# A graph network on one core: the five VectorE instructions of a step's block operands, whole or in halves

## The chip, the core and the metric

The kernel runs on one core of one Trainium2 chip. The metric is device time in microseconds for one execution of the whole program; lower is better. Before the change the median of three runs is 948.86 us (948.36 to 949.64).

## The reference, cut to what matters

Four graph layers run one after the other on 3125 nodes with 128 features. The list has 53,125 edges, sorted by destination. Layer 0 computes a message per edge and sums it by destination; layers 1 to 3 sum node rows over the same edges, unweighted in layers 1 and 3 and weighted by `edge_weight` in layer 2.

```python
h = jnp.maximum(_layernorm(x), 0.0)
msg_in = jnp.concatenate([x[src], x[dst], edge_attr], axis=-1)        # layer 0, x here is h
msgs = jnp.maximum(msg_in @ mW1 + mb1, 0.0) @ mW2 + mb2
agg = jax.ops.segment_sum(msgs, dst, num_segments=num_nodes)          # and so on, an MLP and a norm
...
aggr = jax.ops.segment_sum(gathered, edge_dst, num_segments=n)        # layer 1: x @ W1 + b1 + aggr @ W2 + b2
msgs = norm[:, None] * xw[row]                                        # layer 2: norm = dinv[row] * ew * dinv[col]
agg = jax.ops.segment_sum(x[src] * norm[:, None], dst, num_segments=n)  # layer 3, norm from counts alone
```

## The kernel before, in words

The program has three stages. First a set-up loads and normalises the nodes, multiplies them by the message weights (the table `p_rows` in device memory) and sorts out the edges. Then comes **the sweep** over the edges, 104 steps `q` of 512 edges ("quads"). Last comes the dense stage, in which layers 1 to 3 are products of node rows with dense matrices of edge counts and weights, built during the sweep.

A step of the sweep does two jobs.

- **Messages of layer 0.** GpSimd issues four indirect DMAs (`rows_at`, L769), each of which gathers 128 rows of `p_rows` into one of six buffers `G`. It waits only for a buffer to come free. TensorE's `pre(q)` (L1714, L1715) waits for the four gathers, adds the rows up with the destination's part; ScalarE applies a relu (L927); TensorE's `seg(q)` (L1728) sums the messages by destination with a one-hot matrix from VectorE (`onehot`, L1276); VectorE adds the result into `ST` (`add`, L1263).
- **Blocks of the dense matrices.** For step `u = q - 4` of 100, `block_operands(u)` on VectorE makes the operands of eight blocks, in bf16: a mask `mov[:, k, 0]` that compares block columns (L1287), a mask `sta` that compares block rows (L1290), and three products of the first mask with parts of the edge weights (L1294). They lie in one of three sets `k`. TensorE's `blocks(u, 0)` and `blocks(u, 1)` (L1745, L1747) multiply four blocks each; ScalarE reads them (L952, L957) and they are stored. VectorE makes the operands of `u` in its iteration `q = u + 2`, and TensorE uses them in its iteration `q = u + 4`.

From q = 57 on, TensorE, ScalarE and VectorE also do the rest of layer 0 in pieces (`piece_A`, `piece_U`, `piece_V`, L1760 to L1774), one piece in every four steps. The order on each engine is written out by hand; engines meet at semaphores. `s_bop` counts the block operands that are ready and `s_wmm` the halves that TensorE has used. Before the change, `link` puts a wait on VectorE's own semaphore `s_dve` behind the first mask.

A last part, `again`, runs the layers in another way for edge lists that the sweep can't take; it is jumped over for these inputs.

Of the kernel before, what the change touches and what calls it, by code (L numbers as in the profile page):

```python
# [5 lines left out]
def gnn_kernel(nc, x_in, src_in, dst_in, ea_in, ew_in, mW1, mb1, mW2, mb2, uW1, ub1, uW2, ub2,  # L6
# [4 lines left out]
    ALU = mybir.AluOpType  # L11
# [7 lines left out]
    NT = -(-N // 128)  # L19
# [4 lines left out]
    PARTS = 3  # L24
# [7 lines left out]
    PAD_DST = 3135  # L32
# [11 lines left out]
    STEPS = NP // 32  # L44
    CB = 8
    NW = CB // 2
    KCOLS = 4 * NT
# [44 lines left out]
    with ctx:  # L92
# [3 lines left out]
        def sem(name):  # L96
            return ctx.enter_context(nc.semaphore(name))
# [258 lines left out]
        s_R = sem("messages_ready")  # L356
        s_seg = sem("quad_in_psum")
        s_add = sem("quad_added")
        s_bop = sem("block_operands")
        s_cev = sem("counts_read")  # L360
        s_wmm = sem("weights_in_psum")
# [156 lines left out]
        def _(sp):  # L518
# [165 lines left out]
            with sp.Else():  # L684
                sp.dma_start(x[:, 0:NT - 1, :], x_in[0:128 * (NT - 1), :].rearrange("(t p) d -> p t d", p=128))\
                    .then_inc(s_xc[0], 16)
                sp.wait_ge(z_set, 1)
                sp.dma_start(x[0:NR, NT - 1, :], x_in[128 * (NT - 1):N, :]).then_inc(s_xc[0], 16)
                for i in range(2):
                    sp.dma_start(z_wc[:, i, :], mW1[2 * D + i:2 * D + i + 1, :].to_broadcast([128, D])).then_inc(z_ld, 16)  # L690
                sp.dma_start(z_mb, mb1.rearrange("(a d) -> a d", a=1).to_broadcast([128, D])).then_inc(z_ld, 16)
                whole_c = E // 128
                for c0 in range(0, whole_c, 64):
                    c1 = min(c0 + 64, whole_c)
                    for to, of in ((z_dsti, dst_in), (z_w, ew_in)):
                        sp.dma_start(to[:, c0:c1], of[128 * c0:128 * c1].rearrange("(c p) -> p c", p=128),
                                     allow_slow_non_contiguous=True)\
                            .then_inc(z_ld, 16)
                    sp.dma_start(z_ea[:, c0:c1, :], ea_in[128 * c0:128 * c1, :].rearrange("(c p) i -> p c i", p=128))\
# [12 lines left out]
                sp.dma_start(deg_tab[0:1, 0:NP], ST[0:1, :]).then_inc(s_dst4, 16)  # L712
                sp.dma_start(deg_tab[1:2, 0:NP], ST[1:2, :]).then_inc(s_dst4, 16)
                sp.dma_start(deg_tab[2:3, 0:NP], invb[0:1, :]).then_inc(s_dst4, 16)
                sp.dma_start(deg_tab[3:4, 0:NP], aggT[0:1, :]).then_inc(s_dst4, 16)
                sp.wait_ge(s_dst4, 128)
                load_degrees(sp, 1)
                for s, tile, ready in ((2, h, s_rows[2]), (3, h, s_rows[3]), (4, g3, s_rows[4])):
                    sp.wait_ge(ready, seen(s, 1, NC - 1))
                    sp.dma_start(row_tabs[s].rearrange("(t p) d -> p t d", p=128), tile[:, :, :])\  # L720
                        .then_inc(z_kst, 16)
                store_out(1)
# [3 lines left out]
        def _(pool):  # L726
# [64 lines left out]
                    .then_inc(s_lo, 1)  # L791

            pool.wait_ge(s_oh, NQ)
            pool.wait_ge(s_bop, STEPS)
            widen_group(1, 0)
            pool.wait_ge(s_pre, NQ)
            widen_group(1, 1)
# [48 lines left out]
        def _(act):  # L846
# [270 lines left out]
            with act.Else():  # L1117
                act.wait_ge(s_out, 16 * NC)
                pipeline((0, root(0, 1)), (1, rows(0, 1, h, ACT.Relu, x)), (2, read_T0(1)), (3, store_P_again))
                for j in range(NC):  # L1120
                    act.wait_ge(mm["Q"], j + 1)
                    if j >= 2:
                        act.wait_ge(z_qst, 16 * j)
                    act.activation(z_st[:, j % 2, 0:width(j)], bank(6 + j % 2, width(j)), ACT.Copy).then_inc(ev["Q"], 1)

                def again_sums(s):
                    for j in range(NC):
                        act.wait_ge(z_mm, (s + 1) * NCH + 1)
                        act.activation(part_of(ST, j), bank(j, width(j)), ACT.Copy).then_inc(z_acc, 1)

                again_sums(0)
                again_sums(1)
                layer0()
                again_sums(2)
                pipeline((0, root(3, 1)), (1, rows(3, 1, h, ACT.Relu, x)))
                again_sums(3)
                pipeline((0, root(4, 1)), (1, scaled_rows(1)))
                for j in range(NC):
                    late_part(1, j)
                again_sums(4)  # L1140

        @block.vector
        def _(dve):
            links = [0]

            def link(ins):
                links[0] += 1
                ins.then_inc(s_dve, 1)
                dve.wait_ge(s_dve, links[0])
# [126 lines left out]
                    last = dve.tensor_scalar(oh[:, q % OS, c, :], iota[:, :], dstT[:, q, c:c + 1], None, ALU.is_equal)  # L1276
                last.then_inc(s_oh, 1)

            def blocks_of(a, u, n):
                return a[:, CB * u:CB * u + CB].rearrange("p (i a t) -> p i a t", a=1, t=2)\  # L1280
                    .to_broadcast([128, NW, n, 2])

            def block_operands(u):
                if u >= SETS:
                    dve.wait_ge(s_wmm, 2 * (u - SETS + 1))
                k = u % SETS
                link(dve.tensor_tensor(mov[:, k, 0, :, :, :],  # L1287
                                       iota_k[:, :, :].rearrange("p (a c) t -> p a c t", a=1)
                                       .to_broadcast([128, NW, KCOLS, 2]), blocks_of(Kt, u, KCOLS), ALU.is_equal))
                dve.tensor_tensor(sta[:, k, :, :, :],  # L1290
                                  iota_l[:, :, :].rearrange("p (a c) t -> p a c t", a=1)
                                  .to_broadcast([128, NW, 128, 2]), blocks_of(LOt, u, 128), ALU.is_equal)
                for a in range(PARTS):
                    last = dve.tensor_tensor(mov[:, k, 1 + a, :, :, :], mov[:, k, 0, :, :, :],  # L1294
                                             blocks_of(Wp[:, a, :], u, KCOLS), ALU.mult)
                last.then_inc(s_bop, 1)

            def unpack():
                dve.wait_ge(s_win, 16 * GROUPS)
# [285 lines left out]
                dve.sem_inc(z_set, 1)  # L1585
            with dve.Else():
                dve.wait_ge(s_out, 16 * NC)
                dve.memset(x[:, NT - 1, :], 0.0).then_inc(z_set, 1)
                dve.memset(z_dsti[:, NCH - 1:NCH], PAD_DST).then_inc(z_set, 1)
                dve.memset(z_w[:, NCH - 1:NCH], 0.0).then_inc(z_set, 1)  # L1590
                dve.memset(z_ea[:, NCH - 1:NCH, :], 0.0).then_inc(z_set, 1)
                dve.wait_ge(s_xc[0], 48)
                pipeline((0, variance(0, 1, x)), (1, norm(0, 1)))
                dve.wait_ge(z_ld, 16 * NLOADS)
                dve.wait_ge(z_set, 5)
                link(dve.tensor_copy(z_dstf, z_dsti))
                link(dve.memset(z_R, 0.0))
                link(dve.memset(z_R[:, 0:1], 1.0))
# [48 lines left out]
        def _(pe):  # L1647
# [82 lines left out]
                last.then_inc(s_seg, 1)  # L1730

            def blocks(u, hh):
                if hh == 0:
                    pe.wait_ge(s_bop, u + 1)
                    if u == 0:
                        pe.wait_ge(s_kev, 3)
                        pe.wait_ge(s_flag, 1)
                if u >= 1:
                    pe.wait_ge(s_cev, 2 * u + hh - 1)
                    pe.wait_ge(s_wev, 2 * u + hh - 1)  # L1740
                k = u % SETS
                for b in range(NW):
                    i, t = (NW * hh + b) // 2, b % 2
                    lo, to = sta[:, k, i, :, t], block_out(hh)[:, b, 0:2 * KCOLS]
                    pe.matmul(to.rearrange("p (a c) -> p a c", a=2), lo, mov[:, k, 0:2, i, :, t], start=True, stop=False)  # L1745
                    for a in range(1, PARTS):
                        weighed = pe.matmul(to[:, KCOLS:2 * KCOLS], lo, mov[:, k, 1 + a, i, :, t],  # L1747
                                            start=False, stop=a == PARTS - 1)
                weighed.then_inc(s_wmm, 1)
# [272 lines left out]
```

## Time and profile before

| | |
|---|---|
| median of 3 runs | 948.86 us (948.36 to 949.64) |
| span of the profiled execution | 946.8 us |
| outside the span, against the median | 2.1 us |
| sweep: first gather to last `seg` | about 41 to 624 us |
| TensorE, share of the span | 90% |
| VectorE | 67% |
| ScalarE | 54% |
| GpSimd | 55% |

Of the profiled execution only the span is known; its own time outside the profile is taken as that of the three runs. A view of groups gives, for each line of the kernel, the busy time, the mean duration of one instruction, and the idle time before it with what ended that idle time. The chain of waits is followed back from the end of the program, so it says what set the time at each moment. On VectorE consecutive instructions overlap by some 0.08 us in the records, so what one costs the engine is the distance between two starts, which is less than its duration.

### The profile page before, as it was taken

The page shows a single profiled execution, that of the slowest core. Times are in us where ns is not written, and L with a number is a line of the kernel's source. Part 1 is how long each engine was busy: PE and PEld are TensorE (multiplying, and loading weights), DVE is VectorE, ACT ScalarE, POOL GpSimd, SP SyncE. Part 2 cuts the span into 40 slices and gives each one's busy share as a digit, 9 for nine tenths or more (in the row PEclk, how much of TensorE's full clock was granted, in tenths as well). Part 3 has the DMA queues.
Part 4 walks back from the last instruction along what each step waited for, and adds up shares of the span by engine and source line. Part 5 has one row for each costly group of instructions (what it writes and reads, how often), then busy time and mean ns, then how long its engine had stood idle before and what let it go on. Part 6 is the DMA issues. An engine that isn't in the chain of part 4 may idle for free.

```text
span 946.8 us, 19062 instructions
## 1 busy us (share of the span) xinstructions
PE 851.2 (90%) x6997; PEld 788.9 (83%) x6997; DVE 636.1 (67%) x1758; ACT 510.7 (54%) x1013; POOL 520.9 (55%) x496
## 2 busy tenths in 40 slices
PE   3257889889898978999989999999999999999997
PEld 2257879879898978989989999987889888888886
DVE  6528979887786877779897989968743311115664
ACT  2224757556575656768777788853353011114873
POOL 5477777777777777777777777745110000023110
PEclk9667999999898989999999999999999999999999
DMA  8752556556565666556565556656247778784500
GB/s 206 199 109 71 159 160 209 165 159 214 174 200 158 173 142 192 165 165 204 168 184 156 176 159 196 176 172 195 70 157 274 295 297 299 297 287 139 165 23 27
DMA packets 109503, 168.91 MB, mean 178 GB/s; under 512 B 14723, under 2 KB 69545, under 8 KB 109406
## 3 DMA queue, kind: packets, MB, share of 16 engines
q1 hardware_dynamic: 92062, 137.01, 44.8%
q0 software_dynamic: 13648, 28.21, 11.5%
q10 hardware_dynamic: 3696, 2.42, 0.9%
q8 instruction: 59, 0.97, 0.4%
q14 instruction: 38, 0.31, 0.1%
HBM read 109.15 MB, written 58.44 MB: 177 GB/s over the span
## 4 chain that ended last, share of the span: by engine, by line
PE 43%; POOL 38%; issue 13%; DMA 4%; ACT 1%; SPq 1%; DVE 1%; ACTq 0%; POOLq 0%; DVEq 0%
POOL room L769 36%; PE ps L1889 14%; PE ps L1874 14%; PE ps L1714 2%; DMA room<-p_rows,idx 2%; PE ps L1715 2%; PE ps L1728 2%; PE ps L1858 2%; PE ps L1745 2%; PE ps L1747 2%; PE ps L1650 1%; DMA w_m<-in_L_gnn_mW 1%; POOL pair L769 1%; DMA p_rows<-g 1%; ACTq L905 0%
## 5 line engine op out<-in xcount | busy, mean ns | idle before, releaser
L769 POOL DMA_INDIRECT room<-p_rows,idx x416 | 438.0, 1053 | 137.5 <-issue 125.0
L1714 PE MATMUL ps<-room,ident 128*128 128x128 f32 x832 | 178.8, 299 | 59.7 <-DMA room<-p_rows,idx 58.9
L1714 PEld LDWEIGHTS ps<-room,ident 128*128 128x128 f32 x832 | 135.5, 205 | 63.5 <-DMA room<-p_rows,idx 45.6
L1715 PE MATMUL ps<-room 128*128 128x128 f32 x832 | 170.6, 289 | 0.0
L1745 PE MATMUL ps<-room 128*128 128x200 bf16 x800 | 161.3, 253 | 0.0
L1747 PE MATMUL ps<-room 128*128 128x100 bf16 x1600 | 160.6, 208 | 0.0
L1294 DVE TENSOR_TENSOR room<-room,Wp 128x800 bf16<-128x800 bf16 x300 | 155.4, 571 | 0.0
L1747 PEld LDWEIGHTS ps<-room 128*128 128x128 bf16 x1600 | 147.9, 98 | 3.9
L1889 PE MATMUL ps<-room,h 128*128 128x256 f32 (+1 forms) x650 | 136.2, 371 | 0.0
L1715 PEld LDWEIGHTS ps<-room 128*128 128x128 f32 x832 | 136.0, 205 | 0.0
L927 ACT ACTIVATE g<-ps 128x512 f32<-128x512 f32 x104 | 62.2, 598 | 136.8 <-PE ps L1715 136.7
L1889 PEld LDWEIGHTS ps<-room,h 128*128 128x128 f32 x650 | 119.2, 190 | 15.2
L952 ACT ACTIVATE room<-ps 128x400 uint8<-128x400 f32 x200 | 100.1, 501 | 34.6 <-PE ps L1747 31.9
L1728 PE MATMUL ps<-g 128*128 128x128 f32 x832 | 117.6, 285 | 0.0
L1874 PE MATMUL ps<-wide_room,parts 128*128 128x512 f32 (+1 forms) x520 | 114.7, 375 | 0.0
L1874 PEld LDWEIGHTS ps<-wide_room,parts 128*128 128x128 f32 x520 | 91.1, 188 | 18.1 <-POOL wide_room L474 0.9
L1728 PEld LDWEIGHTS ps<-g 128*128 128x128 f32 x832 | 102.4, 194 | 0.0
L957 ACT ACTIVATE room<-ps 128x400 f32<-128x400 f32 x200 | 100.6, 503 | 0.0
L1263 DVE TENSOR_TENSOR ST<-ST,ps 128x128 f32<-128x128 f32 x104 | 29.1, 279 | 104.8 <-PE ps L1701 70.7
L1276 DVE TENSOR_SCALAR g<-iota,dstT 128x128 f32<-128x128 f32 x416 | 92.2, 299 | 0.0
L870 ACT ACTIVATE sd<-mv,eps 128x2 f32<-128x2 f32 (+3 forms) x45 | 13.5, 301 | 140.2 <-DVE mv L1164 140.2
L933 ACT ACTIVATE room<-room,npio 125x512 bf16<-125x512 bf16 x104 | 75.7, 728 | 17.3 <-DMA room<-dst_row 17.3
(195 smaller groups left out, 1132.1 us busy)
## 6 DMA issues: line engine op xcount, KB each, us to landing
weight_blocks<-room SPq DMA_DIRECT2D x50, 800.0 KB, 4.6
room<-weight_blocks SPq DMA_DIRECT2D x12, 3200.0 KB
room<-dst_row SPq DMA_DIRECT2D x52, 256.0 KB
room<-count_blocks SPq DMA_DIRECT2D x8, 1600.0 KB
count_blocks<-room SPq DMA_DIRECT2D x50, 200.0 KB
room<-p_rows,idx POOLq DMA_INDIRECT x416
first_c<-count_blocks SPq DMA_DIRECT2D x4, 1600.0 KB, 10.0
edge_windows<-room SPq DMA_DIRECT2D x1, 3072.0 KB
```

The costliest lines, as they stand in the source:

```text
L769: return pool.indirect_dma_start(to, None, table, bass.IndirectOffsetOnAxis(ap=at, axis=0))
L952: act.activation(cnt_out[:, u % OUTS, :, at16].rearrange("p h (b w) -> p b h w", w=4), of, ACT.Copy)\
L957: act.activation(w_out[:, u % OUTS, :, at16].rearrange("p h (b w) -> p b h w", w=4), of, ACT.Copy)\
L1276: last = dve.tensor_scalar(oh[:, q % OS, c, :], iota[:, :], dstT[:, q, c:c + 1], None, ALU.is_equal)
L1294: last = dve.tensor_tensor(mov[:, k, 1 + a, :, :, :], mov[:, k, 0, :, :, :], blocks_of(Wp[:, a, :], u, KCOLS), ALU.mult)
L1714: pe.matmul(to, ident[:, :], G[:, n % GS, c, :], start=True, stop=False)
L1715: last = pe.matmul(to, sT[:, n % TS, 128 * c:128 * c + 128], Qr[:, n % QS, :], start=False, stop=True)
L1728: last = pe.matmul(bank(2 + n % 2, 128), R[:, n % RS, c, :], oh[:, n % OS, c, :], start=c == 0, stop=c == 3)
L1745: pe.matmul(to.rearrange("p (a c) -> p a c", a=2), lo, mov[:, k, 0:2, i, :, t], start=True, stop=False)
L1747: weighed = pe.matmul(to[:, KCOLS:2 * KCOLS], lo, mov[:, k, 1 + a, i, :, t], start=False, stop=a == PARTS - 1)
L1874: last = pe.matmul(to, Hr[:, t, a, :], at[:, k, 0:n], start=a == 0 and t == 0, stop=a == 1 and t == NT - 1)
L1889: last = pe.matmul(bank(dense_bank(j))[:, 256 * half:256 * half + 32 * c], h[:, t, :], ring_w[(2 * j + half) % 3][:, 0:c, t, :], start=t = ...
```

## The change

Each of the five instructions becomes two, over four blocks each. Their order is: first mask for half 0, for half 1; second mask for half 0, for half 1; three products of half 0; three products of half 1. Both first masks count up a new semaphore, and the products of a half wait for the mask of their half; the wait between the first and the second mask is gone. `s_bop` is counted up twice in a step, and each of TensorE's `blocks(u, hh)` waits for its own half. The semaphores of the part that is jumped over are renumbered, without effect here.

```diff
+        s_mask = sem("block_masks")
...
-            pool.wait_ge(s_bop, STEPS)
+            pool.wait_ge(s_bop, 2 * STEPS)
...
-                k = u % SETS
-                link(dve.tensor_tensor(mov[:, k, 0, :, :, :],
-                                       iota_k[:, :, :].rearrange("p (a c) t -> p a c t", a=1)
-                                       .to_broadcast([128, NW, KCOLS, 2]), blocks_of(Kt, u, KCOLS), ALU.is_equal))
-                dve.tensor_tensor(sta[:, k, :, :, :],
...
-                for a in range(PARTS):
-                    last = dve.tensor_tensor(mov[:, k, 1 + a, :, :, :], mov[:, k, 0, :, :, :],
-                                             blocks_of(Wp[:, a, :], u, KCOLS), ALU.mult)
-                last.then_inc(s_bop, 1)
+                k, h2 = u % SETS, NW // 2
+                halves = [slice(h2 * half, h2 * half + h2) for half in range(2)]
...
+                for at in halves:
+                    dve.tensor_tensor(mov[:, k, 0, at, :, :],
...
+                        .then_inc(s_mask, 1)
+                for at in halves:
+                    dve.tensor_tensor(sta[:, k, at, :, :],
...
+                for half, at in enumerate(halves):
+                    dve.wait_ge(s_mask, 2 * u + half + 1)
+                    for a in range(PARTS):
+                        last = dve.tensor_tensor(mov[:, k, 1 + a, at, :, :], mov[:, k, 0, at, :, :],
+                                                 blocks_half(Wp[:, a, :], KCOLS, at), ALU.mult)
+                    last.then_inc(s_bop, 1)
...
             def blocks(u, hh):
+                pe.wait_ge(s_bop, 2 * u + hh + 1)
                 if hh == 0:
-                    pe.wait_ge(s_bop, u + 1)
```

On VectorE, one step in the middle of the sweep is this before the change (`room` is the memory that holds `mov` and `sta`; `quad_added`, `q_window_in_psum`, `messages_in_psum` and `quad_in_psum` are semaphores of the message job, `weights_in_psum` is `s_wmm`, `dve_chain` is `s_dve`):

```order
L1263 TENSOR_TENSOR ST<-ST,ps 128x128 [waits quad_added,q_window_in_psum]
L1270 COPY room<-ps 125x128 [waits messages_in_psum,q_window_in_psum]
L1276 TENSOR_SCALAR g<-iota,dstT 128x128 [waits quad_in_psum]
L1276 TENSOR_SCALAR g<-iota,dstT 128x128 x3
L1287 TENSOR_TENSOR room<-iota_k,Kt 128x800 [waits weights_in_psum]
L1290 TENSOR_TENSOR room<-iota_l,LOt 128x1024 [waits dve_chain]
L1294 TENSOR_TENSOR room<-room,Wp 128x800 x3
```

The same step of VectorE after the change, where lines have moved by 2 to 9:

```order
L1265 TENSOR_TENSOR ST<-ST,ps 128x128 [waits quad_added,q_window_in_psum]
L1272 COPY room<-ps 125x128 [waits messages_in_psum,q_window_in_psum]
L1278 TENSOR_SCALAR g<-iota,dstT 128x128 [waits quad_in_psum]
L1278 TENSOR_SCALAR g<-iota,dstT 128x128 x3
L1292 TENSOR_TENSOR room<-iota_k,Kt 128x400 [waits weights_in_psum]
L1292 TENSOR_TENSOR room<-iota_k,Kt 128x400
L1297 TENSOR_TENSOR room<-iota_l,LOt 128x512 x2
L1303 TENSOR_TENSOR room<-room,Wp 128x400 [waits block_masks]
L1303 TENSOR_TENSOR room<-room,Wp 128x400 x2
L1303 TENSOR_TENSOR room<-room,Wp 128x400 [waits block_masks]
L1303 TENSOR_TENSOR room<-room,Wp 128x400 x2
```

Five instructions with one wait on the engine itself have become ten with two such waits, at a later place; nothing else of the step has moved.

On TensorE, this is `seg` with what follows it and the start of the second half, before the change:

```order
L1728 MATMUL ps<-g 128x128 [waits quad_added,q_window_ready,onehot_ready,messages_ready]
L1728 MATMUL ps<-g 128x128 x3
L1701 MATMUL ps<-w_m,hT 128x128
L1745 MATMUL ps<-room 128x200 [waits weights_read,counts_read]
L1747 MATMUL ps<-room 128x100 x2
```

And after it:

```order
L1737 MATMUL ps<-g 128x128 [waits quad_added,q_window_ready,onehot_ready,messages_ready]
L1737 MATMUL ps<-g 128x128 x3
L1710 MATMUL ps<-w_m,hT 128x128
L1754 MATMUL ps<-room 128x200 [waits weights_read,counts_read,block_operands]
L1756 MATMUL ps<-room 128x100 x2
```

The order is the same; the first product of the second half has a third semaphore to wait for.

## Rows read from the trace of the kernel before

**Rows 1.** Page, parts 1 and 4: busy time of engines, the chain that ended last.

```profile
PE 851.2 (90%) x6997; PEld 788.9 (83%) x6997; DVE 636.1 (67%) x1758; ACT 510.7 (54%) x1013; POOL 520.9 (55%) x496
...
PE 43%; POOL 38%; issue 13%; DMA 4%; ACT 1%; SPq 1%; DVE 1%; ACTq 0%; POOLq 0%; DVEq 0%
```

**Rows 2.** Chain of waits around the end of the sweep: start us, us, what.

```profile
489.22 0.30 issue
489.53 7.50 DMA room<-p_rows,idx
...
506.82 0.96 PE ps L1728 x8
...
527.66 0.96 PE ps L1728 x8
...
613.12 4.20 DMA room<-p_rows,idx
617.37 0.49 PE ps L1714 x2
```

**Rows 3.** Who waited for whom: engine, line, releaser, us in total, times, longest.

```profile
POOL room L769 <- issue: 125.0, 410, 0.3
...
PE ps L1714 <- DMA room<-p_rows,idx: 58.9, 19, 16.4
...
POOL room L769 <- PE ps L1715: 1.5, 5, 0.3
```

**Rows 4.** GpSimd's groups, stretch 70 to 366, then 366 to 614.1.

```profile
L769 POOL DMA_INDIRECT room<-p_rows,idx x216 | 231.1, 1070 | 65.8 <-issue 64.3 <-PE ps L1715 1.5
```

```profile
L769 POOL DMA_INDIRECT room<-p_rows,idx x185 | 192.2, 1039 | 56.4 <-issue 56.4
```

**Rows 5.** Line L769: duration ns, min, median and max.

```profile
L769 POOL DMA_INDIRECT room<-p_rows,idx x416: 941/947/3783, 40.8 to 613.1; - x139
```

**Rows 6.** VectorE in order of time: start us, us, instruction.

```profile
222.49 0.69 DVE L1290 TENSOR_TENSOR room<-iota_l,LOt 128x1024 bf16<-128x1024 bf16 x1
223.10 1.54 DVE L1294 TENSOR_TENSOR room<-room,Wp 128x800 bf16<-128x800 bf16 x3
...
225.59 0.86 DVE L1276 TENSOR_SCALAR g<-iota,dstT 128x128 f32<-128x128 f32 x4
226.37 0.57 DVE L1287 TENSOR_TENSOR room<-iota_k,Kt 128x800 bf16<-128x800 bf16 x1
226.97 0.69 DVE L1290 TENSOR_TENSOR room<-iota_l,LOt 128x1024 bf16<-128x1024 bf16 x1
227.58 1.54 DVE L1294 TENSOR_TENSOR room<-room,Wp 128x800 bf16<-128x800 bf16 x3
```

**Rows 7.** GpSimd in the same stretch.

```profile
222.90 1.11 POOL L769 DMA_INDIRECT room<-p_rows,idx  x1 [0.31 <-issue]
224.31 1.15 POOL L769 DMA_INDIRECT room<-p_rows,idx  x1 [0.30 <-issue]
225.76 0.95 POOL L769 DMA_INDIRECT room<-p_rows,idx  x1 [0.30 <-issue]
227.01 1.47 POOL L769 DMA_INDIRECT room<-p_rows,idx  x1 [0.30 <-issue]
```

**Rows 8.** Chain of waits, three long gathers of GpSimd.

```profile
237.07 1.82 POOL room L769
...
313.37 3.78 POOL room L769
...
334.58 3.66 POOL room L769
```

**Rows 9.** TensorE in order of time, two steps in a row.

```profile
296.36 1.12 PE L1728 MATMUL ps<-g 128*128 128x128 f32 x8
300.84 1.12 PE L1728 MATMUL ps<-g 128*128 128x128 f32 x8
```

**Rows 10.** Engines' busy time in 500 to 600: PE, PEld, DVE, ACT, POOL, clock, DMA.

```profile
500.00:600.00 100.00, 100.00 (x1036) 95.32 (x1036) 87.08 (x279) 80.37 (x178) 77.30 (x75) 1.00 0.57 172
```

**Rows 11.** VectorE's waits in 500 to 600.

```profile
DVE ST L1263 <- PE ps L1767: 8.9, 5, 5.6
DVE ST L1263 <- PE ps L1761: 4.5, 5, 0.9
```

More of the change, by code:

```diff
@@ L686, in _ @@
                     .then_inc(s_xc[0], 16)
-                sp.wait_ge(z_set, 1)
+                sp.wait_ge(s_pad, 11)
                 sp.dma_start(x[0:NR, NT - 1, :], x_in[128 * (NT - 1):N, :]).then_inc(s_xc[0], 16)
@@ L1131, in _ @@
                 again_sums(0)
+                act.wait_ge(s_dst4, 128)
                 again_sums(1)
@@ L1277, in onehot @@
                 last.then_inc(s_oh, 1)
-            def blocks_of(a, u, n):
-                return a[:, CB * u:CB * u + CB].rearrange("p (i a t) -> p i a t", a=1, t=2)\
-                    .to_broadcast([128, NW, n, 2])
             def block_operands(u):
@@ L1285, in block_operands, with blocks_half @@
                     dve.wait_ge(s_wmm, 2 * (u - SETS + 1))
-                k = u % SETS
-                link(dve.tensor_tensor(mov[:, k, 0, :, :, :],
-                                       iota_k[:, :, :].rearrange("p (a c) t -> p a c t", a=1)
-                                       .to_broadcast([128, NW, KCOLS, 2]), blocks_of(Kt, u, KCOLS), ALU.is_equal))
-                dve.tensor_tensor(sta[:, k, :, :, :],
-                                  iota_l[:, :, :].rearrange("p (a c) t -> p a c t", a=1)
-                                  .to_broadcast([128, NW, 128, 2]), blocks_of(LOt, u, 128), ALU.is_equal)
-                for a in range(PARTS):
-                    last = dve.tensor_tensor(mov[:, k, 1 + a, :, :, :], mov[:, k, 0, :, :, :],
-                                             blocks_of(Wp[:, a, :], u, KCOLS), ALU.mult)
-                last.then_inc(s_bop, 1)
+                k, h2 = u % SETS, NW // 2
+                halves = [slice(h2 * half, h2 * half + h2) for half in range(2)]
+                def blocks_half(a, n, at):
+                    return a[:, CB * u + 2 * at.start:CB * u + 2 * at.stop].rearrange("p (i a t) -> p i a t", a=1, t=2)\
+                        .to_broadcast([128, h2, n, 2])
+                for at in halves:
+                    dve.tensor_tensor(mov[:, k, 0, at, :, :],
+                                      iota_k[:, :, :].rearrange("p (a c) t -> p a c t", a=1)
+                                      .to_broadcast([128, h2, KCOLS, 2]), blocks_half(Kt, KCOLS, at), ALU.is_equal)\
+                        .then_inc(s_mask, 1)
+                for at in halves:
+                    dve.tensor_tensor(sta[:, k, at, :, :],
+                                      iota_l[:, :, :].rearrange("p (a c) t -> p a c t", a=1)
+                                      .to_broadcast([128, h2, 128, 2]), blocks_half(LOt, 128, at), ALU.is_equal)
+                for half, at in enumerate(halves):
[4 more added lines that the diff above has]
+                    last.then_inc(s_bop, 1)
             def unpack():
@@ L1587, in _ @@
                 dve.wait_ge(s_out, 16 * NC)
[L1588 to L1591, printed above, removed]
+                dve.memset(x[:, NT - 1, :], 0.0).then_inc(s_pad, 1)
+                dve.memset(z_dsti[:, NCH - 1:NCH], PAD_DST).then_inc(s_pad, 1)
+                dve.memset(z_w[:, NCH - 1:NCH], 0.0).then_inc(s_pad, 1)
+                dve.memset(z_ea[:, NCH - 1:NCH, :], 0.0).then_inc(s_pad, 1)
                 dve.wait_ge(s_xc[0], 48)
@@ L1594, in _ @@
                 dve.wait_ge(z_ld, 16 * NLOADS)
-                dve.wait_ge(z_set, 5)
+                dve.wait_ge(z_set, 1)
                 link(dve.tensor_copy(z_dstf, z_dsti))
```

## The prediction

> **What bounds the kernel now.** I began with the page. TensorE is busy for 90% of the span and VectorE for 67%, yet the chain that ended last gives TensorE only 43% of the span, and GpSimd's work 38% with 13% of "issue" beside it [rows 1]. So in about half of the span the time is set by GpSimd, which does little else there than issue the gathers. The waits say the same from the other side: TensorE stood 58.9 us for gathered rows to land, GpSimd stood 1.5 us in all for a free buffer, and 125.0 us of its idle time is a fixed 0.30 us between two gathers [rows 3]. GpSimd therefore runs through the sweep at its own pace. No wait of TensorE for a VectorE product of the blocks is among the costly ones; the operands are made in iteration u + 2 and used in u + 4.
>
> The chain around the sweep's end has three pieces [rows 2]: GpSimd up to a gather issued at 489.53 that took 7.50 us, then TensorE from step to step, and at the end again the last gather, issued at 613.12, which took 4.20 us and for which TensorE's last `pre` waited until 617.37. TensorE's own pace is 4.48 us a step before q = 57 (300.84 - 296.36) [rows 9] and (527.66 - 506.82) / 4 = 5.21 us with the pieces of layer 0 [rows 2]. GpSimd's pace is (231.1 + 65.8) / 54 = 5.50 us a step in 70 to 366, and (192.2 + 56.4) / 46.25 = 5.38 in 366 to 614 [rows 4]. The slower of the two is GpSimd in both parts: by 1.0 us a step in the first, but by only 0.16 in the second, that is 7.6 us over 46 steps.
>
> **What GpSimd waits for.** A gather takes 0.947 us in the median, but 1.070 and 1.039 in the mean [rows 4, 5]: 26.5 us (231.1 - 216 x 0.947) and 17.0 us (192.2 - 185 x 0.947) beyond the median. Beside VectorE's times [rows 6, 7] a pattern shows. The gather of 222.90 begins while L1290 (to 223.18) runs, and ends at 224.01, 0.83 behind it. That of 224.31 begins within the last L1294 (to 224.64) and ends 0.82 behind it. That of 227.01 meets L1290 (to 227.66) and ends 0.82 behind it, though the next VectorE instruction began at 227.58. That of 225.76, among the short L1276, took 0.95. So a gather that starts within such a VectorE instruction stands until this one instruction ends, then needs 0.82 us; it is let through between two in a row. It waits if the instruction has more than 0.947 - 0.82 = 0.13 us left.
>
> The Trainium skill, SBUF — State Buffer, "Who interferes with whom", says that a VectorE instruction with two SBUF inputs blocks a GpSimd instruction that reads SBUF, for the whole instruction; the trace agrees in these rows, where both inputs are in SBUF.
>
> **The change, part by part.**
>
> *GpSimd.* An instruction of duration d has a window of d - 0.13 in which a gather's start is held, on average by half of it, so the wait goes with the square of the window. Before: four of 0.44 (0.57 - 0.13) and one of 0.56 (0.69 - 0.13): (4 x 0.19 + 0.31) / 2 = 0.54. Half the size: 224 columns are 0.12 to 0.13 us (0.69 - 0.57), so 400 fewer take 0.22 off and 512 fewer 0.29: 0.35 and 0.40 long, windows 0.22 and 0.27. After: (8 x 0.048 + 2 x 0.073) / 2 = 0.27. The waits on these instructions halve.
> How large are they? From 43.5 us I take what longer instructions cause: the two gathers of 3.78 and 3.66 (5.5 us), and those like the 1.82 one, of which there are four as `block_degrees` runs four times (3.5 us) [rows 8]. That leaves 17.5 in the first part and 17.0 in the second. The four L1276 (0.28 each, windows of 0.15) have 0.05 against 0.54, some 10%. So 15.7 and 15.3 us hang on the five, and halving saves 7.8 and 7.6, together **15.4 us of GpSimd's time**.
>
> *VectorE.* From the starts in [rows 6]: L1290 costs 0.61 us (226.97 to 227.58), the first mask 0.60 with its wait (226.37 to 226.97), and three L1294 in 1.54 - 0.57 are 0.485 apart. Extrapolated from 800 and 1024 columns the fixed cost of one is 0.485 - 800 x 0.125 / 224 = 0.04 us. It can't be under nothing, and the nearest short row is L1276: (0.86 - 0.28) / 3 = 0.19 for 128 columns of fp32 all told, the upper bound. I take 0.04 to 0.07. Five more instructions are 0.2 to 0.35 us a step; the dropped wait gives 0.11 back (0.60 - 0.485). Net +0.1 to +0.24 us. Its cover is VectorE's idle time. In 500 to 600 it is 87% busy [rows 10] and waits 13.4 us, of which one wait of 5.6 belongs to the late gather; the other 7.8 us over the 18 steps are 0.43 a step [rows 11]. So 0.2 is left, and cost nothing. In the first part the pace leaves TensorE 1.0 us a step, and VectorE, which follows it, has that on top.
> The Trainium skill, Perfetto Trace Analysis, "Optimizing Scalar/DVE Operations", speaks against the change: some 60 ns of overhead for each VectorE instruction, so rather grouped. By its figure, an estimate, VectorE's step would grow by 5 x 0.06 - 0.11 = 0.19 us, within my range and under the idle time.
>
> *TensorE.* One more semaphore on 100 products that already wait for two. The halves come earlier, but TensorE wasn't waiting. I take 0; bounds 0 and 0.05 us a step.
>
> *The sum.* First part: TensorE is far from its limit, so all 7.8 us arrive. Second part: GpSimd would come to 5.38 - 7.6 / 46 = 5.21, level with TensorE. At best it gives 7.6. But when both have one pace, a gather that lands late is not made up for: that of 489.53 was 3.3 us later than the last one (7.50 against 4.20), which before was hidden by the 0.16 us a step. At worst it gives 7.6 - 3.3 = 4.3. So 12.1 to 15.4, I take 13.4. Against the profiled span that is 946.8 to 933.4; with the 2.1 us between span and median, 948.9 to **935.5 us**. The dense stage, some 320 us behind the sweep, is not touched.
>
> **The rivals.**
>
> *No change in GpSimd's waits (about 949).* The wait could go with the time for which VectorE holds what both want, not with one instruction: then two halves hold it as long as the whole. For it: I have it from a few coincidences. Against it: at 227.01 GpSimd got in between two instructions with no gap between them. VectorE's extra 0.1 to 0.24 us stays hidden, so 948 to 951.
> The Trainium skill, SBUF — State Buffer, in the same section, infers that descriptor generation needs only the write side, so that `tensor_tensor` would not stall it; by that the split would give nothing, and the rows on 1.11 and 1.47 us speak against it.
>
> *The gain ends up in TensorE (about 943).* If further late gathers or a lower granted clock take the second part's gain and some of the first's, 4 to 7 us remain: 942 to 945. For it: TensorE is 100% busy in 500 to 600 [rows 10]. Against it: in the first part it has 1 us a step to spare.
>
> *VectorE becomes the bound (slower, about 965).* The mechanism is a fixed cost per instruction near the upper bound, 0.19. The step grows by 5 x 0.19 - 0.11 = 0.84, over the 0.43 of idle time: 0.41 x 46 = 19 us over TensorE's 46 x 5.21 = 240, so 259 against 46 x 5.38 = 248, 11 slower. Halves would then last 0.5, GpSimd's windows 0.37 eight times and 0.43 twice, 0.73 against 0.54, and the first part would lose 15.7 x 0.35 = 5.5: some 16 us in all. It decides from (0.43 + 0.11) / 5 = 0.11 us an instruction on. Against it: two sizes of the same instruction give 0.04.
>
> **How the numbers follow.** 0.2% of 949, 1.9 us, is about what a measurement can tell from no change. The forecast (929 to 942) has 0.71. The gain that ends in TensorE has 0.08, no change in the waits 0.12, VectorE as the bound 0.09. Faster: 0.71 + 0.08 = 0.79; same 0.12; slower 0.09. The range begins at 929, since 15.4 us are all that halving can give and some clock and landing times may improve with it, and goes up to 948, which leaves out the slower case, most of "no change" and a little below 929, in all some 0.2.
>
> **What would show it.** The mean of L769 falls from 1053 ns in the page's groups to about 1015, its median stays at 947, no gather among block operands is above 1.25, and GpSimd's last gather is issued near 598 instead of 613. The ten VectorE instructions are 0.35 and 0.40 us long and start 0.26 to 0.28 and 0.32 to 0.34 apart; VectorE still waits for TensorE in 500 to 600, and TensorE never for the block operands. I'd be wrong if L769 keeps its mean, if VectorE's waits are gone, or if the gathers speed up and TensorE's steps grow.

## The result: 1098 us, 16% slower

The changed kernel takes 1098.16 us in the median of 4 runs (1092.3 to 1105.73), against 949.25 for the kernel before in the same comparison. The ratio is 1.156, 95% interval 1.150 to 1.161. I had forecast 935.5 and gave "slower" 0.09. The times below leave out three slow runs: one of `mask_halves` (2180.56 us), one of the kernel before (2989.71 us) and one of `whole_pause_after_copy` (1040.98 us; the ratio of 1.085 in the table counts it, and the medians without it give 1.078).

From the page of the changed kernel: the span, part 1 and a row of part 5, beside [rows 1] (a line may have moved: L769 is L770 now, L1714 is L1723):

```profile
span 1102.1 us, 19562 instructions
...
PE 898.8 (82%) x6997; PEld 828.8 (75%) x6997; DVE 662.5 (60%) x2258; ACT 512.9 (47%) x1013; POOL 671.3 (61%) x496
...
L770 POOL DMA_INDIRECT room<-p_rows,idx x416 | 589.0, 1416 | 137.9 <-issue 124.4
```

The 416 gathers have 589.0 us of GpSimd's time, 1416 ns each. Before, their mean was 1070 ns in the first and 1039 in the second part [rows 4], in all 438.0 us. That is 151.0 us more, of the 155.3 by which the span grew, and the last gather is issued at 764.97 instead of 613.12 [rows 2], 151.9 us later:

```profile
764.97 3.52 DMA room<-p_rows,idx
768.54 0.49 PE ps L1723 x2
```

The fixed "issue" time between the gathers is as it was [rows 3]. Who waited for whom, and the single gathers (min, median, max in ns):

```profile
PE ps L1723 <- DMA room<-p_rows,idx: 165.4, 54, 17.2
...
L770 POOL DMA_INDIRECT room<-p_rows,idx x416: 940/947/3792, 41.6 to 765.0; - x139
```

TensorE waits 165.4 us for gathered rows, where it waited 58.9 [rows 3], and none of its waits is put down to the block operands. The median gather is 0.947 us as before [rows 5]. So most gathers are as fast as ever and some are very slow.

TensorE's clock fell too. In the sweep, before and after (engines as in [rows 10], the clock behind the five busy times):

```profile
70.00:614.00 544.00, 497.95 (x5104) 482.49 (x5105) 451.43 (x1283) 372.30 (x776) 422.14 (x400) 0.96 0.58 171
```

```profile
70.00:766.00 696.00, 545.56 (x5117) 522.76 (x5117) 478.64 (x1785) 375.35 (x778) 574.02 (x401) 0.89 0.44 134
```

The mean granted clock is 0.89 instead of 0.96, and TensorE's matmuls take 47.6 us more. It is busy for 78% of the stretch instead of 92%, standing still for gathered rows in between, so this slower clock did not set the pace.

GpSimd (first) and VectorE in order of time, beside [rows 6, 7]:

```profile
303.28 0.94 POOL L770 DMA_INDIRECT room<-p_rows,idx  x1 [0.30 <-issue]
304.53 3.30 POOL L770 DMA_INDIRECT room<-p_rows,idx  x1 [0.30 <-issue]
308.14 0.94 POOL L770 DMA_INDIRECT room<-p_rows,idx  x1 [0.30 <-issue]
```

```profile
303.20 1.07 DVE L1278 TENSOR_SCALAR g<-iota,dstT 128x128 f32<-128x128 f32 x4
304.05 0.63 DVE L1292 TENSOR_TENSOR room<-iota_k,Kt 128x400 bf16<-128x400 bf16 x2
304.60 0.75 DVE L1297 TENSOR_TENSOR room<-iota_l,LOt 128x512 bf16<-128x512 bf16 x2
305.27 1.74 DVE L1303 TENSOR_TENSOR room<-room,Wp 128x400 bf16<-128x400 bf16 x6
```

The gather of 304.53 begins within the second half of the first mask. It ends at 307.83. The row of ten block instructions ends at 305.27 + 1.74 = 307.01, and 307.83 is 0.82 behind that. The 0.82 is the time that I had read from [rows 6, 7], but what it counts from is now the end of all ten instructions and not of the one that was met.

### The profile page after: what moved, and what is told of

The parts are those of the page before. It is cut to its first block and busy times, and to the rows that moved or that the text cites. A ratio compares the mean times of both kernels' runs of the same rounds, so it can differ in the third digit from the quotient of the medians.

```text
span 1102.1 us, 19562 instructions
## 1 busy us (share of the span) xinstructions
PE 898.8 (82%) x6997; PEld 828.8 (75%) x6997; DVE 662.5 (60%) x2258; ACT 512.9 (47%) x1013; POOL 671.3 (61%) x496
## 5 line engine op out<-in xcount | busy, mean ns | idle before, releaser
L770 POOL DMA_INDIRECT room<-p_rows,idx x416 | 589.0, 1416 | 137.9 <-issue 124.4
L1723 PE MATMUL ps<-room,ident 128*128 128x128 f32 x832 | 196.2, 323 | 166.1 <-DMA room<-p_rows,idx 165.4
L1723 PEld LDWEIGHTS ps<-room,ident 128*128 128x128 f32 x832 | 149.5, 225 | 175.5 <-DMA room<-p_rows,idx 156.6
L1724 PE MATMUL ps<-room 128*128 128x128 f32 x832 | 186.7, 312 | 0.0
L1303 DVE TENSOR_TENSOR room<-room,Wp 128x400 bf16<-128x400 bf16 x600 | 175.1, 363 | 0.0
L1265 DVE TENSOR_TENSOR ST<-ST,ps 128x128 f32<-128x128 f32 x104 | 29.6, 284 | 236.1 <-PE ps L1710 157.5
L1754 PE MATMUL ps<-room 128*128 128x200 bf16 x800 | 169.4, 262 | 0.0
L1756 PE MATMUL ps<-room 128*128 128x100 bf16 x1600 | 168.6, 213 | 0.0
L1756 PEld LDWEIGHTS ps<-room 128*128 128x128 bf16 x1600 | 153.9, 101 | 6.0
L1724 PEld LDWEIGHTS ps<-room 128*128 128x128 f32 x832 | 151.5, 227 | 0.0
L791 POOL TENSOR_TENSOR parts<-g,parts 128x512 fp32r<-128x512 f32 x5 | 6.4, 1272 | 130.4 <-ACT parts L1051 130.4
L1754 PEld LDWEIGHTS ps<-room 128*128 128x128 bf16 x800 | 81.7, 102 | 3.9 <-issue 3.6
```

The costliest lines, as they stand in the source:

```text
L770: return pool.indirect_dma_start(to, None, table, bass.IndirectOffsetOnAxis(ap=at, axis=0))
L1303: last = dve.tensor_tensor(mov[:, k, 1 + a, at, :, :], mov[:, k, 0, at, :, :], blocks_half(Wp[:, a, :], KCOLS, at), ALU.mult)
L1723: pe.matmul(to, ident[:, :], G[:, n % GS, c, :], start=True, stop=False)
L1724: last = pe.matmul(to, sT[:, n % TS, 128 * c:128 * c + 128], Qr[:, n % QS, :], start=False, stop=True)
```

## The experiments

The ratios below are to the kernel before on the same chip, with 95% intervals. "Waits" is 416 x (mean - 0.944 us), from the row of L769 or L770 of each profile; 0.944 us is the median gather in `halves_two_pauses`, where few are held.

| kernel | ratio | mean gather, ns | waits, us |
|---|---|---|---|
| before | 1 | 1053 | 45 |
| changed | 1.156 (1.150 to 1.161) | 1416 | 196 |
| halves_one_wait | 1.146 (1.139 to 1.152) | 1374 | 179 |
| whole_no_gap | 1.120 (1.114 to 1.125) | 1338 | 164 |
| mask_halves | 1.129 (1.119 to 1.139) | 1359 | 173 |
| product_halves | 1.002 (1.000 to 1.005) | 1056 | 47 |
| group_gaps | 0.996 (0.993 to 0.998) | 1010 | 27 |
| whole_pause_and_wait | 1.001 (0.999 to 1.003) | 1050 | 44 |
| whole_pause_before | 1.018 (1.013 to 1.022) | 1086 | 59 |
| halves_one_pause | 1.009 (1.006 to 1.013) | 1073 | 54 |
| mask2_first | 1.049 (1.044 to 1.054) | 1158 | 89 |
| whole_pause_after_copy | 1.085 (1.079 to 1.091) | 1227 | 118 |
| product_quarters | 1.041 (1.033 to 1.049) | 1154 | 87 |
| halves_two_pauses | **0.977 (0.975 to 0.980)** | 996 | 22 |

The time goes with the waits of the gathers. Each kernel's time differs from that of the kernel before by what its waits differ, within 6 us, `product_quarters` (39 and 42 us) and `whole_pause_before` (16 and 14) included. The exception is `group_gaps`: its waits are 18 us shorter, its time only 6; its VectorE is 97% busy in 500 to 600, against 87% before.

### Is it the size, or the row?

In the diffs `mask1(at)`, `mask2(at)` and `product(a, at)` are the instructions of L1287, L1290 and L1294 over the pairs of blocks `at`; the diffs are to the body of `block_operands` in the kernel before, or in the changed kernel where this is said. Each kernel computes the whole reference.

A "pause" is a wait of VectorE for a result of its own that isn't there yet, so that it stands still for a moment (0.03 us between the masks in [rows 6]). The first kernel leaves every instruction whole and only drops the pause:

```diff
-                link(mask1(whole))
+                mask1(whole).then_inc(s_mask, 2)
                 mask2(whole)
+                dve.wait_ge(s_mask, 2 * u + 2)
                 for a in range(PARTS):
                     last = product(a, whole)
```

> Whole instructions as before, but without the wait between the first and the second mask; the products wait for the mask instead, as in the changed kernel. Theory LINE-UP (a gather that meets a row of VectorE instructions with no pause between them stands until the row ends, once enough of them follow): the row is now five long, a gather caught in the first mask stands up to 2.7 us, the mean gather goes from 1.05 to 1.2 us or more and the time to 990 us or more. Theory SIZE (what keeps a gather out is that the instructions are short; between instructions of 0.56 us or more it gets in): gather mean 1.05 us, longest wait by the block instructions under 0.6 us, time 945 to 951 us.

It took 1068 us. A gather of it and the instructions of VectorE around:

```profile
148.49 3.39 POOL L770 DMA_INDIRECT room<-p_rows,idx  x1 [0.30 <-issue]
```

```profile
148.44 0.57 DVE L1288 TENSOR_TENSOR room<-iota_k,Kt 128x800 bf16<-128x800 bf16 x1
148.92 0.68 DVE L1294 TENSOR_TENSOR room<-iota_l,LOt 128x1024 bf16<-128x1024 bf16 x1
149.53 1.54 DVE L1299 TENSOR_TENSOR room<-room,Wp 128x800 bf16<-128x800 bf16 x3
```

The gather met the whole first mask at 148.49 and ended at 151.88, which is 0.81 behind the end of the last product (151.07). SIZE falls: at 0.57 and 0.68 us the same happens. 116 of the 149 us come without a single halved instruction.

The second and third halve one kind only. `product_halves` keeps the pause behind the first mask; `mask_halves` has none.

```diff
                 mask1(whole).then_inc(s_mask, 2)
                 dve.wait_ge(s_mask, 2 * u + 2)
                 mask2(whole)
-                for a in range(PARTS):
-                    last = product(a, whole)
+                for at in halves:
+                    for a in range(PARTS):
+                        last = product(a, at)
```

> Masks whole with the pause behind the first, as before; only the three products are halved, six in a row behind the second mask. LINE-UP: seven in a row without a pause, so gathers caught in the second mask or the first products stand up to 2.3 us; mean 1.25 us or more, time over 1000 us. SIZE: a gather caught in the second mask gets in behind it, one caught in a product stands to the end of the six, up to 1.7 us; mean near 1.2 us, time 980 to 1020 us. If neither (no gather waits over 0.6 us), the halved masks are what matters.

953 us, the mean gather 1056 ns. Seven instructions in a row follow the pause, and every gather got in behind the one that it met. So both theories were wrong here: how many instructions follow does not decide.

```diff
-                link(mask1(whole))
-                mask2(whole)
+                for at in halves:
+                    mask1(at).then_inc(s_mask, 1)
+                for at in halves:
+                    mask2(at)
+                dve.wait_ge(s_mask, 2 * u + 2)
```

> Both masks halved (four instructions of 0.36 to 0.42 us, no pause), products whole behind them. LINE-UP: seven in a row, as bad as the product halves or worse, over 1000 us. SIZE: a gather caught in a half mask stands to the end of the four, about 1.2 us, and gets in between whole products; mean near 1.1 us, time 955 to 980 us.

1076 us. Its time agrees with LINE-UP, but after `product_halves` that theory could not stand. What the three slow kernels (changed, `whole_no_gap`, `mask_halves`) have in common, and `product_halves` has not, is the lost pause.

`group_gaps` is the changed kernel with a pause behind each group:

```diff
                 for at in halves:
                     mask1(at).then_inc(s_mask, 1)
+                dve.wait_ge(s_mask, 2 * u + 2)
                 mask2(halves[0])
-                mask2(halves[1])
+                link(mask2(halves[1]))
                 for half, at in enumerate(halves):
-                    dve.wait_ge(s_mask, 2 * u + half + 1)
...
                     last.then_inc(s_bop, 1)
+                    dve.wait_ge(s_bop, 2 * u + half + 1)
```

> All ten halves as in the changed kernel, with VectorE waiting for its own last result behind every group (2 first masks, 2 second masks, 3 products, 3 products). LINE-UP with a row of at most three: gathers get in at every boundary, mean 1.0 us, time 935 to 950 us. SIZE: gathers stand to the end of their group, at most 1.0 us; mean 1.06 to 1.1 us, time 945 to 970 us. Either way far below the 1098 us of the changed kernel; if it stays above 1050, the pauses do not matter and both theories fall.

946 us, a little under the kernel before. Four pauses turn 1.156 into 0.996, all ten halves being kept. The waits ahead of the products are gone here too; the next kernel and `halves_one_pause`, which keeps them, show that they are not what counts.

### Where must the pause be, and does a wait in the row matter?

The changed kernel also has a wait that is met in advance, ahead of the products. `whole_pause_and_wait` keeps the pause and adds such a wait:

```diff
-                link(mask1(whole))
-                mask2(whole)
-                for a in range(PARTS):
-                    last = product(a, whole)
+                mask1(whole).then_inc(s_mask, 1)
+                dve.wait_ge(s_mask, 2 * u + 1)
+                mask2(whole).then_inc(s_mask, 1)
+                product(0, whole)
+                dve.wait_ge(s_mask, 2 * u + 2)
+                product(1, whole)
+                last = product(2, whole)
```

> Whole instructions with the pause behind the first mask, as before the change; new is a wait of the second product for the second mask, that is for the instruction but one ahead of it, as the changed kernel's products wait for their mask. Theory PAUSE (gathers get in between VectorE instructions only in a row that VectorE began after standing still; a row that runs on from the one-hots without a pause shuts them out): the gathers are as before, mean 1.05 us, longest by the block instructions under 0.6 us, time 945 to 953 us. Theory MET WAIT (a wait in the row for an earlier instruction of the same row shuts out the gathers that came before it): those caught in the second mask stand to the end of the row, 2 us, mean 1.2 us or more, time over 1000 us.

`whole_pause_before` is `whole_no_gap` with a pause ahead of the first mask:

```diff
+                dve.wait_ge(s_oh, min(u + 4, NQ))
                 mask1(whole).then_inc(s_mask, 2)
                 mask2(whole)
```

> Whole instructions, no pause behind the first mask and the met wait ahead of the products, as in the run that took 1068 us; new is a pause ahead of the first mask, where VectorE waits for its own last one-hot. PAUSE: the row begins after standing still, so gathers get in at every boundary, mean 1.05 us, 945 to 955 us. MET WAIT: nothing is mended, 1040 us or more.

951 and 967 us. The met wait does nothing. The pause works from ahead of the masks too, though this kernel came out above the 945 to 955 expected: only one gather at a block instruction was kept beyond the one that it met, yet the mean is 1086 ns. The gathers that met a product and got in behind it stood 25.6 us in all, against 14.2 before. Why they stood longer is only argued: a gather that is let in behind one instruction begins the next at a fixed distance, and here falls in with a worse phase.

`halves_one_pause` is the changed kernel with one pause put back, between the two first half masks:

```diff
+                mask1(halves[0]).then_inc(s_mask, 1)
+                dve.wait_ge(s_mask, 2 * u + 1)
+                mask1(halves[1]).then_inc(s_mask, 1)
```

> The changed kernel with one thing put back: VectorE waits for the first half mask before the second. All else is as in the changed kernel. PAUSE: a gather caught by any half gets in behind it; mean 0.99 to 1.04 us, longest by the block instructions under 0.5 us, time 935 to 950 us. MET WAIT: gathers caught in the first four instructions are still shut out, over 1040 us.

959 us, so one pause in a step takes 139 of the 149 us away. It missed its range of 935 to 950 by 9.

`mask2_first` is `whole_no_gap` with the masks in the other order, so that the wait of the products is a pause:

```diff
-                mask1(whole).then_inc(s_mask, 2)
                 mask2(whole)
+                mask1(whole).then_inc(s_mask, 2)
                 dve.wait_ge(s_mask, 2 * u + 2)
```

> Whole instructions in the order second mask, first mask, pause (the products wait for the instruction right ahead), products. PAUSE: a gather caught in the first of the row stands to the end of the second, at most 1.1 us; from the pause on it gets in everywhere; mean 1.06 to 1.12 us, time 948 to 975 us. MET WAIT: the wait is one that is not met in advance, as before the change, so about the same prediction, not higher than 975 us. If it comes out over 1020 us both fall: the order or the instruction ahead of the one-hots matters.

994 us, above its range. Of the 44 us by which the waits are longer than before, some 25 are of 31 gathers that met the second mask ahead and stood to the pause behind the first. Another 17 are of gathers that met a product and got in behind it: they stood 31.3 us in all, against 14.2 before.

### Counting in the row

For each gather that met a block instruction with more than 0.13 us left, I looked up in the starts and durations of the trace how many VectorE instructions had run since VectorE last stood still, and whether the gather ended 0.82 us behind the one that it met ("in") or later ("out"). Gathers that were not held at all, the last block instruction of a step and any instruction right ahead of a pause are left out: behind these nothing holds a gather for long, or in and out can't be told apart. So are positions beyond the eleventh.

```
kernel                   position since VectorE stood still: in/out
before                   1: 26/0   3: 22/0
product_halves           1: 64/0   3: 22/0   4: 8/0    6: 68/0
whole_pause_and_wait     1: 28/0   3: 16/0
whole_pause_before       1: 33/0   2: 31/0   3: 7/0    4: 35/1   5: 1/0    10: 1/0
halves_one_pause         1: 12/0   2: 12/0   3: 19/0   4: 43/0   7: 17/6   8: 3/16
group_gaps               1: 39/0   2: 26/0   7: 0/11
mask2_first              2: 9/0    7: 5/7    8: 2/8    9: 2/2    10: 0/14
changed                  3: 1/0    5: 1/1    7: 2/9    8: 0/10   9: 4/21   10: 0/7   11: 0/3
whole_no_gap             2: 1/0    3: 5/0    4: 0/1    7: 4/7    8: 7/14   9: 7/10   10: 4/6   11: 2/0
mask_halves              3: 1/0    4: 1/0    5: 0/1    6: 1/0    7: 13/3   8: 0/5    9: 0/30   10: 0/9   11: 17/4
```

Up to the sixth nearly all got in, from the seventh on most did not; but the 13 of 16 at the seventh in `mask_halves` did. The sixth rests almost wholly on `product_halves`, where only one block instruction is left behind it. In the changed kernel the row begins with `add` (L1265), the copy and four one-hots, so that the first half mask is already the seventh.

The pause also helps at once. Of the 46 gathers of the kernel before that met L1290, the instruction right behind the pause, the 16 that began within 0.041 us of its start were not held at all, and the mask lasted 0.73 to 0.77 us instead of 0.69; those from 0.046 us on with more than 0.13 us of it left were held to its end:

```profile
231.45 0.76 DVE L1290 TENSOR_TENSOR room<-iota_l,LOt 128x1024 bf16<-128x1024 bf16 x1
```

```profile
231.49 0.95 POOL L769 DMA_INDIRECT room<-p_rows,idx  x1 [0.31 <-issue]
```

Three kernels test what the count suggests. The first is `halves_one_pause` with a second pause:

```diff
                     last.then_inc(s_bop, 1)
+                    if half == 0:
+                        dve.wait_ge(s_bop, 2 * u + 1)
```

> The changed kernel with two pauses of VectorE: behind the first half mask and behind the first half's products, so that no row of VectorE instructions without a pause has more than seven, and of its block instructions only the one that a pause follows stands seventh. Theory COUNT (a gather gets in behind the instruction it met if that is among the first six since VectorE last stood still; from the seventh on it mostly stands to the row's end): with one pause, gathers that met the eighth and ninth instruction still stood to the end; here none does, no gather stands over 0.5 us at the block instructions, mean 0.99 to 1.03 us, time 938 to 950 us. Rival (one pause behind the masks is enough and the 959 us with one pause come from VectorE's added time): a second pause costs VectorE 0.1 us more, 958 to 965 us.

931 us: the fastest of all, 2.3% under the kernel before. No gather stood over 0.5 us at a block instruction, as expected; the range of 938 to 950 us was missed by 7, to the good.

`product_quarters` is `product_halves` with four slices in place of two:

```diff
-                for at in halves:
+                for i in range(NW):
                     for a in range(PARTS):
-                        last = product(a, at)
+                        last = product(a, slice(i, i + 1))
```

> Masks whole with the pause behind the first, as before; the three products in quarters, so twelve short ones follow the second mask, thirteen in a row without a pause and without any wait in the row. COUNT (position in the row alone decides): gathers that met one of the first five or six get in behind it, those that met the seventh to tenth stand up to 1.2 us, to the row's end. Rival (a wait inside the row is needed to shut them out; in all rows that did so there was one): every gather gets in behind the instruction that it met, none over 0.6 us at the block instructions. The time says little here, since VectorE has some 0.6 us more a step: 950 to 990 us.

990 us. For the products COUNT holds, and the rival falls. The twelve products begin at 160.90, 0.17 apart; the gather of 162.10 met the seventh of them, the eighth since the pause, and stood until 163.06, the end of the twelve, plus 0.81:

```profile
162.10 1.77 POOL L770 DMA_INDIRECT room<-p_rows,idx  x1 [0.30 <-issue]
```

```profile
160.29 0.69 DVE L1294 TENSOR_TENSOR room<-iota_l,LOt 128x1024 bf16<-128x1024 bf16 x1
160.90 2.16 DVE L1299 TENSOR_TENSOR room<-room,Wp 128x200 bf16<-128x200 bf16 x12
162.98 0.28 DVE L1265 TENSOR_TENSOR ST<-ST,ps 128x128 f32<-128x128 f32 x1
```

VectorE did not stand still behind the twelve: `add` began at 162.98, before the last product had ended. So what ends such a wait is the end of the block instructions, and not a standstill.

All 28 gathers that met the seventh product stood 0.8 us or more, while the 72 that met the third or fourth product (the fourth and fifth since the pause) stood 0.05 at most.

`whole_pause_after_copy` is `whole_no_gap` with a pause in `onehot`:

```diff
             def onehot(q):
+                if q:
+                    dve.wait_ge(s_Qr, min(q + 3, NQ))
                 for c in range(4):
```

> Whole instructions with no pause behind the first mask (that took 1068 us); new is a pause ahead of the four one-hots, well away from the masks. COUNT: the first mask is now the fifth since VectorE stood still and the second the sixth, so gathers that met these get in behind them, where before they stood up to 2.5 us; mean 1.05 to 1.15 us, time 950 to 985 us. Rival (a pause helps only where it is next to the masks): 1040 us or more, waits of 2.5 us remain.

1026 us. Better than without the pause (1068), but far above the 950 to 985 expected. Gathers that met the first mask, the fifth since the pause, got in 24 times and stayed out 10; those at the second mask, the sixth, 1 and 15. So the number is not the whole rule, and a limit of six is not one either. In the kernels without a pause behind the first mask, gathers that met one of the last two or three of the row also got in again: all that met the second product did, 25 at position 8 in `whole_pause_after_copy` and 4 at position 10 in `whole_no_gap`, and in the changed kernel the 4 at position 9 met the ninth half. The count does not explain that, nor that in `product_quarters`, at the products with two or one behind them, 71 of 72 gathers did not. How VectorE and GpSimd pass on what both want is open. What is shown is that taking the standstill away shuts gathers out for whole rows and putting it back lets most of them in. For how many instructions it helps is known only roughly.

### TensorE's part

In the changed kernel:

```diff
-                pe.wait_ge(s_bop, 2 * u + hh + 1)
                 if hh == 0:
+                    pe.wait_ge(s_bop, 2 * u + 2)
```

> The changed kernel, but TensorE waits once a step for both halves. Theory COUNT puts the whole loss on VectorE's instructions and GpSimd's gathers: 1085 to 1110 us as the changed kernel. Rival (TensorE's wait for the second half costs time): clearly below 1085 us.

1091 us in 2 runs, within the 1085 to 1110 expected. The ratio is 1.146 (1.139 to 1.152), and its interval overlaps that of the changed kernel (1.150 to 1.161). Its gathers wait 179 us instead of 196, which is more than the 8 us between the medians. TensorE's second wait is not the cause of the loss; that it costs up to some 1% isn't excluded.

### The version that beats both

`halves_two_pauses` is the changed kernel and two lines that let VectorE wait for itself. Its page, its waits and its busy time in 500 to 600, beside [rows 10]:

```profile
span 929.6 us, 19662 instructions
...
L770 POOL DMA_INDIRECT room<-p_rows,idx x416 | 414.5, 996 | 138.0 <-issue 123.4
```

```profile
PE ps L1736 <- DMA room<-p_rows,idx: 29.3, 14, 4.9
...
PE ps L1767 <- DVE room L1299: 1.5, 1, 1.5
```

```profile
500.00:600.00 100.00, 100.00 (x1046) 96.02 (x1045) 97.65 (x385) 80.66 (x180) 69.24 (x73) 1.00 0.59 178
```

```profile
L770 POOL DMA_INDIRECT room<-p_rows,idx x416: 940/944/4072, 41.4 to 590.2; - x139
```

The gathers have 23.5 us less than before (438.0 - 414.5) and the last is issued at 590.2 instead of 613.1. TensorE waits half as long for them. VectorE is 98% busy in 500 to 600, so nothing is left there for more instructions. The median fell by 21.4 us (952.09 to 930.68).

## Why the prediction was wrong

- **The bound** was right. GpSimd's gathers set the sweep's pace; they account for 151 of the 155 us, and for the gain of `halves_two_pauses` too (23.5 us less in the gathers, 21.4 in the time).
- **The step that failed** is in "What GpSimd waits for": "a gather that starts within such a VectorE instruction stands until this one instruction ends ... it is let through between two in a row". The rows showed it for instructions that stand first to fourth behind a pause [rows 6, 7]; I took it for a rule on any two instructions. Even there it had an exception, the 16 gathers that came right behind the pause. The runs showed instead that it holds for a few instructions after VectorE has stood still, and that later ones mostly keep the gather out to the end of the block instructions. So the term of 15.4 us saved was 151 us lost.
- **The dropped wait** stood in the sum as a saving, "the dropped wait gives 0.11 back". The 0.11 is right (first mask to next instruction 0.60 before, 0.484 in `whole_no_gap`); what it had done for GpSimd was worth some 116 us.
- **Halving the waits.** What the waits cost before was right: by the starts and durations of the trace, gathers that met one of the five instructions stood 31.1 us in all, and the sum has 15.7 + 15.3. What shorter instructions save was too low once the pauses are there: in `halves_two_pauses` 7.6 us of the 31.1 are left, so 23.5 are saved and not 15.4. That this kernel takes 931 us, near my 935.5 for the changed one, is partly luck: it is another kernel, with two pauses that the sum did not have.
- **VectorE's cost.** Starts are 0.276 and 0.334 apart and the halves last 0.36 and 0.42 us; I had 0.26 to 0.28, 0.32 to 0.34, and 0.35 and 0.40. From 0.276 at 400 columns and 0.484 at 800 the fixed cost of one is 2 x 0.276 - 0.484 = 0.07 us, the upper end of my 0.04 to 0.07. It did not become the bound.
- **TensorE's cost** of nothing for the third semaphore was right within some 1%.
- **The rivals.** None named this. "No change in GpSimd's waits" had the thought that what VectorE holds may be more than one instruction, but let it stay at the old sum. The slower rival had the wrong mechanism and a size of 16 us.
- **The page's rule.** In [rows 7] each gather that was held waited for one instruction; later in a row it was for up to ten, 2.8 us. The Trainium skill, SBUF — State Buffer, "Who interferes with whom", lets the loser wait for "the whole instruction". The runs here disagree for gathers that come late in a row. The same section's inference that `tensor_tensor` would not stall descriptor generation does not hold for these gathers: at the five `tensor_tensor` they stood 31.1 us in all before the change, and single ones up to 2.8 us after it.

## What to carry to other kernels

When an engine gets what it shares with another only between the other's instructions, look at what stands between these before you remove it: a wait that costs 0.1 us may be the gap through which the other engine lives. Before splitting an instruction, count how many run in a row without a standstill, and put a pause back after some five. Its place has to be tried: ahead of the one-hots (`whole_pause_after_copy`) it gave back only 42 of the 116 us. And rows that show a rule show it with their surroundings; here all of them came from just behind a pause.

## What was not expected of the hardware

- A gather that met a late instruction of a row stood up to 2.8 us behind instructions of 0.36 to 0.42 us each, and boundaries between instructions that let others in did not help it: in `product_quarters` the gather that met the seventh product passed five more boundaries.
- A standstill of VectorE of 0.03 us once a step was worth 116 us in 952 (`whole_no_gap` against the kernel before), and 139 us with halves.
- Whole products, halves and the same pause give the same mean gather (1053 and 1056 ns) though the instructions differ by 0.21 us: after being let in, the gathers settle at fixed places of VectorE's step (68 of them at the sixth after the pause in `product_halves`), so that an average over random starts, as in my sum, holds only roughly.
